# Decoder, experts stage: the first shared layer moved ahead of the third batch's transposes, and batch statistics taken one batch ahead of the write-out

## The reference, cut to what matters

```python
scores = sigmoid(xt @ gate.T)
_, sel = top_k(scores + expert_bias, 2)
routed = xt[token_idx] * scores_sorted[:, None]        # two rows a token
h  = silu(xb @ w1e.T) * (xb @ w3e.T);  oe = h @ w2e.T  # of its expert, bf16
hs = silu(xt @ shared_w1.T) * (xt @ shared_w3.T)       # all tokens, float32
out = hs @ shared_w2.T  (+ the two rows of oe)
x = layernorm(x + out)
```

## Time and profile before

| | |
|---|---|
| median of three runs | 2925.47 us (2925.18 to 2925.68) |
| profiled execution | 2926.31 us |
| its span | 2924.0 us |
| TensorE busy | 2618.9 us (90%) |
| VectorE, ScalarE, GpSimd busy | 1987.5, 1464.5, 1215.2 us |
| mean granted TensorE clock | 0.963 of full speed |
| first instruction of the experts on TensorE | 2670.56 us |

### The profile page before, as it was taken

How to read it: one execution, slowest core, us unless ns; L and a number is a source line. 1 busy time by engine, 2 the same in 40 slices (tenths; PEclk the granted TensorE clock), 3 DMA queues, 4 the chain that set the end, 5 groups by cost and what they waited for, 6 DMA issues and landing times. The chain is left out here.

```text
span 2924.0 us, 47477 instructions
## 1 busy us (share of the span) xinstructions
PE 2618.9 (90%) x16941; PEld 1754.4 (60%) x16941; DVE 1987.5 (68%) x2548; ACT 1464.5 (50%) x2868; POOL 1215.2 (42%) x1148
## 2 busy tenths in 40 slices
PE   8999899888888888886999999999998889997986
PEld 5666645544444444443999777777775555555863
DVE  4788757689999999966111169999999833333453
ACT  3444412289999998962222166666666411111510
POOL 0000026446666665643221148678888700000451
PEclk9999999989999999998999999999999999998998
DMA  2123513268888887965012211111112271111273
GB/s 98 53 90 128 202 48 110 68 128 173 170 167 166 170 169 160 191 153 174 30 43 75 94 44 51 59 52 59 58 51 94 78 129 36 40 63 36 82 158 126
DMA packets 537722, 297.99 MB, mean 102 GB/s; under 512 B 444400, under 2 KB 482544, under 8 KB 533680
## 3 DMA queue, kind: packets, MB, share of 16 engines
q1 hardware_dynamic: 520896, 258.50, 35.0%
q0 software_dynamic: 16624, 36.84, 4.2%
HBM read 126.45 MB, written 64.23 MB: 65 GB/s over the span
## 5 line engine op out<-in xcount | busy, mean ns | idle before, releaser
L1188 DVE TENSOR_REDUCE xh_top<-xh_seen 128x1 f32<-128x512 f32 (+1 forms) x768 | 631.6, 864 | 43.8 <-PE xh_seen L1090 30.2
L1160 ACT ACTIVATE xh_prob<-xh_sc,xh_bias,xh_scale 128x1024 int16<-128x1024 f32 (+1 forms) x512 | 610.1, 1202 | 67.1 <-PE xh_sc L1090 66.7
L2335 POOL TENSOR_TENSOR ss_state<-ss_du,ss_b_all 128x1024 f32<-128x1024 f32 x128 | 443.5, 3478 | 172.5 <-PE ss_turned L1933 98.2
L1090 PE MATMUL xh_seen<-xh_kT,xh_qT 96*128 96x512 bf16 x1024 | 353.3, 387 | 80.3 <-DVE xh_top L1188 78.0
L2383 DVE TENSOR_TENSOR_SCAN ss_state<-ss_decay,ss_state 128x1024 f32<-128x1024 f32 x128 | 384.4, 3004 | 27.8 <-ACT ss_decay L2185 27.8
L1090 PE MATMUL xh_sc<-xh_kT,xh_qT 96*128 96x512 bf16 x1024 | 308.6, 383 | 1.4 <-ACT xh_prob L1160 1.3
L1214 POOL CAST xh_probT<-xh_pairs 128x2048 int16<-128x2048 uint8 x128 | 241.9, 1890 | 12.5 <-DMA xh_pairs<-xh_prob 2.7
L1090 PEld LDWEIGHTS xh_seen<-xh_kT,xh_qT 96*128 96x128 bf16 x1024 | 89.2, 97 | 240.8 <-DVE xh_top L1188 219.2
L1940 PE MATMUL ss_bank<-ss_xc,hold_w_conv 128*128 128x256 f32 x1024 | 229.3, 379 | 0.7 <-ACT ss_xc L2197 0.7
L2185 ACT ACTIVATE ss_decay<-ss_delta,ss_a 128x255 f32<-128x255 f32 x512 | 210.6, 495 | 0.4
L1940 PEld LDWEIGHTS ss_bank<-ss_xc,hold_w_conv 128*128 128x128 f32 x1024 | 190.0, 189 | 26.4 <-ACT ss_xc L2197 1.1
(11 more groups left out here) (399 smaller groups left out, 4883.6 us busy)
## 6 DMA issues: line engine op xcount, KB each, us to landing
ex_rows_in<-sa_unused POOLq DMA_DIRECT2D x18, 1088.0 KB, 5.1
ss_b_all<-ss_states SPq DMA_DIRECT2D x8, 2048.0 KB, 7.1
xa_kT<-xp_kT SPq DMA_DIRECT2D x8, 768.0 KB, 5.2
xh_qT<-xa_qT SPq DMA_DIRECT2D x48, 128.0 KB, 3.1
xh_kT<-xa_kT SPq DMA_DIRECT2D x48, 128.0 KB, 3.2
sa_x<-in_x SPq DMA_DIRECT2D x8, 512.0 KB, 3.7
sa_y<-in_x SPq DMA_DIRECT2D x8, 512.0 KB, 6.6
x_after_self_attention<-sa_y_out SPq DMA_DIRECT2D x8, 512.0 KB, 6.1
```

Source lines behind the costliest of these rows:

```text
L1090: ins = pe.matmul(out[:, c * D:(c + 1) * D], qT[s][:, t * P:(t + 1) * P], kT[s][:, at + c * D:at + (c + 1) * D], start=True, stop=True)
L1160: act.activation(out, scores, ACT.Exp, bias=bias[t % RING][:, :], scale=scale[s][:, t:t + 1], accum_out=total[s][:, half, t:t + 1]).then_i ...
L1188: ins = v.tensor_reduce(top[t % RING][:, k:k + 1], scores[:, 0:n], AX.X, ALU.max)\
L2335: g.tensor_tensor(state[k % RING][:, :, :], du[s][:, :, :], spread(b_all[s][:, k, :], KD), ALU.mult)\
```

## The change

In the routing, PE calls `expand_shared(0)` before `turn_input(2)`, not after it. ACT calls `gate_shared(0)` before `front(2)`, and `scale(0)` after `front(3)` instead of before `odds(2)`.

At the end `normal` is split. `gather_moments(n)` takes the statistics up to `shifted`; `normal(n)` waits for the root and writes the batch out. The statistics' results, `shifted` and the root get a second buffer each, used in turn. DVE now calls gather_moments(0), gather_moments(1), normal(0), gather_moments(2), normal(1) and so on. PE's order and its waits are as before.

```diff
         ln = Norm(p)
+        moments = [ln.moments, p.sb("moments1", [P, TB, 2])]
+        shifted = [ln.shifted, p.sb("shifted1", [P, TB])]
+        rstd = [ln.rstd, p.sb("rstd1", [P, TB])]
...
             for n in range(B):
-                inverse_root(g, ln, n)
+                g.wait_ge(ln.shifted_ready, ONE + n + 1)
+                g.tensor_tensor(rstd[n % 2][:, :], shifted[n % 2][:, :], ln.minus_half[:, :], ALU.pow).then_inc(ln.rstd_ready, 1)
...
             pe.wait_ge(s_loaded, ONE + 48)
+            expand_shared(0)
             turn_input(2)
-            expand_shared(0)
             pe.wait_ge(made, ONE + 1)
             count_earlier(0)
...
                 front(n)
                 odds(n)
+            gate_shared(0)
             front(2)
-            gate_shared(0)
-            scale(0)
             odds(2)
             front(3)
+            scale(0)
             scale(1)
             odds(3)
             front(4)
...
-            def normal(n):
+            def gather_moments(n):
                 chain = Chain(v, chain_y, 2, n)
                 v.wait_ge(y_ps, ONE + n + 1)
                 for t in range(TB):
                     ins = v.bn_stats(ln.stats[:, t, :], sums[n % PAIRS][t])
                 chain(ins)
                 for t in range(TB):
-                    ins = v.bn_aggr(ln.moments[:, t, :], ln.stats[:, t, :])
+                    ins = v.bn_aggr(moments[n % 2][:, t, :], ln.stats[:, t, :])
                 chain(ins)
-                v.tensor_scalar(ln.shifted[:, :], ln.moments[:, :, 1], EPS, None, ALU.add).then_inc(ln.shifted_ready, 1)
+                v.tensor_scalar(shifted[n % 2][:, :], moments[n % 2][:, :, 1], EPS, None, ALU.add).then_inc(ln.shifted_ready, 1)
+                chain.end()
+
+            def normal(n):
                 v.wait_ge(ln.rstd_ready, ONE + n + 1)
                 for t in range(TB):
-                    ins = v.tensor_scalar(y_out[n][:, t, :], sums[n % PAIRS][t], ln.moments[:, t, 0:1], ln.rstd[:, t:t + 1],
-                                          ALU.subtract, ALU.mult)
+                    ins = v.tensor_scalar(y_out[n][:, t, :], sums[n % PAIRS][t], moments[n % 2][:, t, 0:1],
+                                          rstd[n % 2][:, t:t + 1], ALU.subtract, ALU.mult)
                 ins.then_inc(y_done, 1)
-                chain.end()
...
             for n in range(B):
-                normal(n)
+                gather_moments(n)
+                if n >= 1:
+                    normal(n - 1)
+            normal(B - 1)
```

## The result

Over 19 runs each, the changed kernel's median is 2933.09 us and that of the kernel before 2926.36 us. The ratio on record is 1.0018, with a 95% interval of 1.0012 to 1.0025: 5.3 us more (3.5 to 7.3). The two medians alone lie 6.7 us apart.

What follows compares the result with a forecast made beforehand. It took PE's idle 7.74 and 4.73 us and a 10.06 us turn to bound the routing, PE's 5.17 us beat the end. -9.6 + 15.0 = +5.4 on the 2925.47 median gave 2930.9 us, range 2925.5 to 2935.0.

Steps and rivals of the forecast that it cites:

- The front: Routing: with the first shared layer moved up, batch 1's shared layer ends at 2711.2 instead of 2720.81, -9.6 us.
- The first layer: Routing: expand_shared(0) starts at 2682.3 behind route(1), takes 8.8 us and ends at 2691.1.
- The second layer: Routing: batch 1's shared layer on PE, at the slow clock, takes 8.7 us and ends at 2711.2.
- The cover: Routing: ACT's silu, table load and scalings, and choose, run hidden beside other work and cost nothing.
- The end: Sums and layer norms: three new PE waits of 3.3 us, a turn of 10.30 against 5.17, +15.0 us.
- G with its step to N: DVE at the end: a batch's statistics up to shifted plus the step to its write-out, 1.71 us together.
- The root: Layer norm: it no longer stalls DVE, running beside a write-out; gives back 0.9 us in each of the last batches.
- A: Routing: first layer or routes stay slow, the gain is under 9.1 us; +9.0 in all, 2934.5; chance 0.15.
- B: Final additions: PE's clock holds through the new waits, cost only +10.1; +0.5 in all, 2926.0; chance 0.10.
- D: Final additions: the three new waits do not come, -1.2 there; faster in all, 2914.7; chance 0.05.
- E: Routing: its gain gets lost in a wait now hidden, a scatter or load; +15, 2940; chance 0.02.
- C: Routing: it runs at full clock, -12.4 there; +2.6 in all, 2928.1; chance 0.07.

Runs made afterwards that it cites:

- kernel 5: The kernel before with the first shared layer ahead of the third batch's transposes and its silu ahead of front(2), scale(0) unmoved: ratio 0.9975.
- kernel 6: The kernel before with only scale(0) moved behind front(3), PE's order and layer norm as before: ratio 0.9996.
- kernel 1: The kernel before with only the whole routing edit, on PE and ACT, and the layer norm as before: ratio 0.9966, 10.0 us faster.
- kernel 3: The changed kernel with DVE's statistics running ahead only where PE has no addition left that waits for a write-out: ratio 0.9955.
- kernel 4: The changed kernel with PE adding the results of batches 2 and 3 before add_shared(4), then add_shared(n), add_results(n): ratio 0.9936, 18.7 us faster.
- kernel 2: The kernel before with only the early statistics at the end, routing as before: ratio 1.0054, 15.8 us slower.
- kernel 8: The changed kernel with its statistics over the first 256 of 512 columns of each token: ratio 1.0001.

## Why the prediction was right, step by step

*The number.* Forecast 5.4 us more, 2930.9; measured 5.3 more by the ratio, and a median of 2933.09. Both mechanisms, the independence of the halves and the near balance came as put. That the two numbers agree to 0.1 us is luck: the parts were off by 0.5 and 1.0 us against each other, and the stretches that the change does not touch moved by 2.6 in the profiled pair. Between same and slower the chances were nearly even (0.50 and 0.44), and the interval, 0.12 to 0.25%, lies on both sides of the 0.2% that was to part them, so it says little about them.

*The front, -9.6 put, -10.1 measured.* The start of the first layer (2682.3) and the rest of the order are as written. Two terms were mis-sized, in opposite ways. The first layer took 9.51 us, above both my 8.8 and the upper row of 9.10: the clock did not rise until about 2687, 5 us into it. The changed kernel's windows:

```profile
2684.00:2686.00 2.00, 2.00 (x6) 1.61 (x5) 1.66 (x11) 0.00 (x0) 0.00 (x0) 0.50 0.69 262
2686.00:2688.00 2.00, 2.00 (x8) 1.65 (x8) 0.83 (x5) 0.00 (x0) 0.00 (x0) 0.76 0.25 60
```

The second layer took 7.60, not 8.7, for the clock rose soon after its start. By the rule that the prediction took from the Trainium skill (TensorE: Matmul & The Clock Gate, Part 4: PE-mode transpose), that transposes do not count as busy work, the gain was to be nearer 8; that did not come. Nor do the rows settle what the transposes do: right behind 1.95 us of slow ones the layer took 7.60 us here, 8.40 in kernel 5 and 9.01 in kernel 6, and right behind a route 9.43 to 9.54. When the clock rises stays open.

*The cover.* The silu, the table load, the two scalings and choose cost nothing, as put: PE's waits between 2682 and 2712 are the two copies of 1.09. That is seen in the changed kernel and in kernels 1, 3 and 4, whose routing stretch is the same to 0.02 us. The table load also waited 0.81 us for `put(0)`, which the prediction had left out; it was covered all the same. The stores cost nothing either: from the end of the last write-out to the end of the span it is 10.82 us in the changed kernel and 10.85 in the kernel before.

*The end, +15.0 put, +16.0 measured.* The wait is 3.3 us, and the turn 10.40 against 10.30. The term that was off is the slow clock: add_shared(4) took 2873.14 - 2866.36 = 6.78 where I had taken the 5.94 of the kernel before, and the others 6.07. Against that, G with its step to N was 1.69, not 1.71, and a pair on DVE 3.12, not 3.15. The Trainium skill (TensorE: Matmul & The Clock Gate, HAM oscillation) has each burst behind such a stall start at the slow rate. The trace agrees in part: in the changed kernel and in kernel 2 each addition behind a new wait ran mostly slow (6.0 to 6.1 us against 4.31), in kernel 8 one of three did not. But in the changed kernel the clock was still full when add_shared(5) began at 2877.47, and fell after that:

```profile
2876.00:2878.00 2.00, 0.53 (x5) 0.53 (x6) 1.42 (x2) 0.00 (x0) 0.69 (x1) 1.00 0.00 0
2878.00:2880.00 2.00, 2.00 (x5) 0.83 (x4) 0.00 (x0) 0.00 (x0) 0.00 (x0) 0.53 0.68 262
```

*The root.* It runs beside the write-out at 0.69. The Trainium skill (SBUF - State Buffer, Who interferes with whom) says that a VectorE instruction with at most one SBUF input does not contend with GpSimd outside the two-port modes, and the trace agrees: the write-out beside it takes 1.52 to 1.53, as it does in series.

*The rivals.* A (front below 9) and B (clock holding in the tail) did not come in the profiles; D and E are excluded by kernels 2 and 1. That the clock can hold through such a wait was seen in kernels 1 and 8, so B's price, about 1.6 us for each wait, was real. C (the front at full clock) did not come: route(3) took 3.58 us and both layers started slow.

## What to carry to other kernels

Moving work earlier on one engine is free only if nothing behind it is what another engine waits for: read for each signal that the moved instruction now precedes what releases the mover, and whether that comes from the very engine which waits for the signal. Here the write-out of a buffer came to stand behind statistics of work that PE issues just before it asks for that buffer, a ring of 10.4 us where there had been slack; putting PE's short additions two batches ahead opened it again, and the same idea then gained. When two edits are measured as one, measure them apart: near zero was -10 and +16.

## What the runs showed of the hardware that I had not expected

The granted clock after a short wait is not fixed by the wait. Behind 3.38 us of idle and the same code, add_shared(4) took 4.37 us (kernel 1), 5.94 (before) and 7.11 (kernel 3); behind 2.77 us, turns of 8.17 and 9.86 stand side by side in kernel 8; and behind only 2.40 us it took 6.05 in kernel 4. A cost taken from one profiled instance of such a stall, 5.94 here, was 1.6 us too high for one kernel and 1.2 too low for another. The rise is as loose: the same 32 matmuls, 7.07 us at full clock, took 7.56 to 9.54 when they started slow. The longest of them ran slow for some 5 us.
